# Split rows of both norms in two buffers each, queries' split moved to step 3, shared expert's down product in plain fp32

## The chip, the cores and the metric

The kernel runs on one core of a Trainium2 chip, written instruction by instruction with explicit semaphores. The metric is device time in microseconds, less is better.

## The reference

A layer without learned weights in its first norm feeds two branches, whose results are added to the input x (8 batches of 256 tokens of 128 values, fp32):

```python
xn = layernorm(x)
x + attention(xn) + ffn(xn)
# attention: a second layernorm with norm_g, norm_b; q from it, k and v from xn;
#   16 heads of 64, q and k scaled to unit length, 2 null keys and values a head,
#   a distance bias by head, causal mask, softmax, product with v, output projection Wout
# ffn: shared = (silu(xt @ sg_w.T) * (xt @ su_w.T)) @ sd_w.T       (128 -> 256 -> 128)
#   routed: sigmoid router, the 2 best of 8 experts, each 128 -> 256 -> 128
```

## The kernel before, in words

A preparation makes the norms, the router and the sorting of tokens by expert (32 scatters by GpSimd), and turns all weights. `xn1T` holds the first norm's result and `xn2T` the second's, both turned so that tokens lie along the free axis, complete before the main loop. Then 39 tiles of 128 routed tokens go through the experts. Then comes the attention loop, one entry per batch: `first` (batch 0), six times `mid`, `last`, and a short `drain`. The loops are unrolled; every engine runs its own copy of `entry(part, b, steps)` in a fixed order with 16 steps, one per head: in step s the scores of head s, the row maxima (DVE L900), the exponentials (ACT L676), the division (DVE L915), the transposes of the probabilities (PE L1111) and so on for heads some steps back.

Between them stand the side jobs, listed by hand in `JOBS` as (step, whose, kind, c, w, t) for two side banks. `kq` makes a half of the queries (w = 1, from `xs2`) or keys (w = 0, from `xs1`) of the next batch, `v` the values, `tr` transposes scaled queries and keys (PE L1066), `sh` is the shared expert's gate and up product, `yt` and `pn` close the batch before. The queries' first product (`kq`, w = 1) stands in step 1, the keys' and values' of the next batch in steps 5, 6, 12 to 15, the values' second half and `sh` of the own batch in steps 4, 5 and 8.

Many products use reduced-precision fp32 (`F32R`) in three matmuls: each operand is split into a rounded upper part and the remainder, and `three` (L969 to L973) adds hi x hi, lo x hi and hi x lo. The split of a batch's rows is two GpSimd instructions of 128x256, a cast and a subtraction (L457 and L460). Before, each of `xs1` and `xs2` has one buffer, so GpSimd makes both in steps 0 (xn2T, the queries) and 1 (xn1T) of the entry before, after the last product that reads the old content. As the own batch still needs xn1T in steps 4 to 8, step 2 splits it once more into `xs_late` (L477, L480). The shared expert's hidden rows `hs` are split in steps 7 and 10 (L468, L470) into `hss`, and the down product of step 13 (PE, after the output projection L1134) accumulates six matmuls into bank 6.

GpSimd also takes the inverse norms of queries and keys (a power of 128x8, L426 or L429), scales the rows by them (L442), copies the null probabilities (L495) and, in step 10, issues four gathers of expert outputs (L506). DVE adds these in the `yt` job (L870, L877). Semaphores count: `xhi` and `xlo` the parts of a split, `filled` and `left` the use of the side banks, `sh_h` the halves of `hs`.

Of the kernel before, what the change touches and what calls it, by code (L numbers as in the profile page):

```python
# [40 lines left out]
def build(nc, a, out):  # L41


    with ExitStack() as ctx:
        def sb(name, shape, dt=F32):
            return ctx.enter_context(nc.sbuf_tensor(name, shape, dt))
# [17 lines left out]
        sd = [sb("sd_hi", [P, 2, DIM], F32R), sb("sd_lo", [P, 2, DIM], F32R)]  # L64
# [57 lines left out]
        arena_r = sb("arena_r", [P, 3072], F32R)  # L122
# [6 lines left out]
        xs1, xs2 = ([carve_r(SEQ), carve_r(SEQ)] for _ in range(2))  # L129
        mxT = [[carve_r(P), carve_r(P)] for _ in range(RH)]  # L130
        mhT = [sb(f"mhT{i}", [P, I]) for i in range(2)]
        rt[0] = 4 * SEQ
        oT = [sb(f"oT{i}", [P, SEQ]) for i in range(2)]
        hss = [carve_r(2 * I), carve_r(2 * I)]
# [8 lines left out]
        xs_late = [sb(f"xs_late{i}", [P, SEQ], F32R) for i in range(2)]  # L143
# [9 lines left out]
        def three_d(n, m):  # L153
# [47 lines left out]
            "xhi", "xlo", "late_hi", "late_lo", "ksq", "red", "ssm_ready", "pw", "r_ready", "kqn",  # L201
            "sh_th", "sh_a", "sh_h", "sh_hi", "sh_lo", "shd",
# [87 lines left out]
        def head_at(part, s, lag):  # L290
# [12 lines left out]
                    [t[:].rearrange("p c d -> p (c d)") for t in sd], "d")]  # L303
# [6 lines left out]
        def settled(eng):  # L310


            eng.sem_inc(g.passed, 1)
# [48 lines left out]
        def _(pool):  # L362
# [80 lines left out]

            def entry(part, b, steps=range(HEADS)):
                whose = PARTS[part]
                nb = b + 1
                for s in steps:
                    if s < 2 and "next" in whose and part != "ready":
                        xT, xs = ((xn2T, xs2), (xn1T, xs1))[s]
                        for _, _, (kind, c, w, t, i, n) in (x for lag in range(1, HEADS) for x in behind(part, b, s, lag)):  # L450
                            if (kind, c, w, t) == (("kq", 1, 1, 1), ("v", 0, 0, 1))[s]:
                                pool.wait_ge(filled[i], n + 1)
                        if part == "first":
                            for i in range(2):
                                pool.wait_ge(filled[i], count("ahead", i) + count("ready", i))
                        settled(pool)
                        gp.tensor_copy(xs[0], xT[:, bass.ds(nb * SEQ, SEQ)]).then_inc(g.xhi, 1)  # L457
                        pool.wait_ge(g.xhi, 2 * nb + s + 1)
                        settled(pool)
                        gp.tensor_tensor(xs[1], xT[:, bass.ds(nb * SEQ, SEQ)], xs[0].bitcast(F32),  # L460
                                         ALU.subtract).then_inc(g.xlo, 1)
                    if s in (7, 10) and "own" in whose:
                        c = (7, 10).index(s)
                        pool.wait_ge(g.sh_h, 2 * b + c + 1)
                        if part != "first":
                            pool.wait_ge(g.shd, b)
                        settled(pool)
                        gp.tensor_copy(hss[0][:, c * SEQ:(c + 1) * SEQ], hs[:, c, :]).then_inc(g.sh_hi, 1)  # L468
                        pool.wait_ge(g.sh_hi, 2 * b + c + 1)
                        gp.tensor_tensor(hss[1][:, c * SEQ:(c + 1) * SEQ], hs[:, c, :],  # L470
                                         hss[0][:, c * SEQ:(c + 1) * SEQ].bitcast(F32), ALU.subtract).then_inc(g.sh_lo, 1)
                    if s == 2 and "own" in whose:
                        for _, _, (kind, c, _, t, i, n) in (x for lag in range(1, HEADS) for x in behind(part, b, s, lag)):
                            if (kind, c) == ("sh", 1):
                                pool.wait_ge(filled[i], n + 1)
                        settled(pool)
                        gp.tensor_copy(xs_late[0][:], xn1T[:, bass.ds(b * SEQ, SEQ)]).then_inc(g.late_hi, 1)  # L477
                        pool.wait_ge(g.late_hi, b + 1)
                        settled(pool)
                        gp.tensor_tensor(xs_late[1][:], xn1T[:, bass.ds(b * SEQ, SEQ)], xs_late[0][:].bitcast(F32),  # L480
                                         ALU.subtract).then_inc(g.late_lo, 1)
                    h = head_at(part, s, 2)
                    for _, job_b, job in (behind(part, b, s, 1) if part != "ahead" else []):
                        norms(job_b, job)
                        scale_by_norm(job_b, job)
                    if h is not None and h % 2:
                        p = h // 2
                        pool.wait_ge(g.pn, TB * (HEADS * b + h + 1))
                        if p == 0 and part != "first":
                            pool.wait_ge(g.pn_hi, 2 * b)  # L490
                        settled(pool)
                        q = p % PAIRS
                        two = prob[:, (HEADS * b + h) % RP - 1:(HEADS * b + h) % RP + 1, :]
# [35 lines left out]
        def _(act):  # L529
# [42 lines left out]
            sc.activation(xs1[0], xn1T[:, 0:SEQ], ACT.Copy).then_inc(g.xhi, 1)  # L572
# [6 lines left out]
            for i in range(8, 12):  # L579
                turned_out(i)  # L580
                if i == 8:
                    act.wait_ge(g.t_ev, 9)
                    sc.activation(xs2[0], xn2T[:, 0:SEQ], ACT.Copy).then_inc(g.xhi, 1)
# [140 lines left out]
        def _(dve):  # L724
# [86 lines left out]
            ve.tensor_tensor(xs1[1], xn1T[:, 0:SEQ], xs1[0].bitcast(F32), ALU.subtract).then_inc(g.xlo, 1)  # L811
# [16 lines left out]
            ve.tensor_tensor(xs2[1], xn2T[:, 0:SEQ], xs2[0].bitcast(F32), ALU.subtract).then_inc(g.xlo, 1)  # L828
# [137 lines left out]
        def _(pe):  # L966
# [82 lines left out]
            def side_job(job, b):  # L1049
# [7 lines left out]
                if kind == "kq":  # L1057
                    pe.wait_ge(g.xlo, 2 if isinstance(b, int) and b < 0 else 2 * nb + 2 - w)
                    ins = three(side[i][:], [x[:, tt] for x in (xs2 if w else xs1)],
                                [x[:, c * 512:(c + 1) * 512] for x in (wq if w else wkv)], True, True)  # L1060
# [6 lines left out]
                if kind == "v":  # L1067
                    if c:
                        pe.wait_ge(g.late_lo, b + 1)
                    else:  # L1070
                        pe.wait_ge(g.xlo, 2 * nb + 2)
                    ins = three(side[i][:], [x[:, tt] for x in (xs_late if c else xs1)],
                                [x[:, INNER + c * 512:INNER + (c + 1) * 512] for x in wkv], True, True)
                if kind == "sh":
                    pe.wait_ge(g.late_lo, b + 1)
                    for gu in range(2):
                        ins = three(side[i][:, gu * SEQ:(gu + 1) * SEQ],
                                    [x[:, (2 * gu + c) * P:(2 * gu + c + 1) * P] for x in sgu], [x[:] for x in xs_late], True, True)
# [10 lines left out]
            def entry(part, b, steps=range(HEADS)):  # L1089
                whose = PARTS[part]  # L1090
                for s in steps:
# [135 lines left out]
```

## Time and profile before

| | |
|---|---|
| median of 3 runs | 491.92 us (491.72 to 493.71) |
| profiled execution | 492.31 us, its span 490.6 us |
| PE / PEld | 86% / 62% of the span |
| DVE / ACT / POOL | 74% / 73% / 65% |
| share of the chain that ended last | PE 35%, POOL 24%, DVE 19%, issue 11%, ACT 7%, DMA 2% |

The profile records one execution. PE is TensorE's matmul, PEld its weight load, DVE VectorE, ACT ScalarE, POOL GpSimd. "x" is the number of instructions; of a plain fp32 matmul two records are shown. The ends of matmuls are modelled, so they can overlap by some tenths of a microsecond. A row of the timeline gives start and length in us, engine, line, operation, the tile written and those read; in brackets the idle time before it and what ended it. arena_b, arena_r and bank are names of storage that several tiles share.

### The profile page before, as it was taken

How to read it: one execution, taken by the hardware profiler on the slowest of the kernel's cores; microseconds unless marked ns; L12 is line 12 of the kernel's file. 1: busy time of each engine (PE TensorE's matmuls, PEld its weight loads, DVE VectorE, ACT ScalarE, POOL GpSimd, SP SyncE). 2: the span in 40 equal slices, each digit the busy share in tenths (PEclk: the TensorE clock that was granted, in tenths of full speed). 3: DMA queues.
4: the chain of work that ended last, by engine and by line, in shares of the span. 5: the costliest groups of instructions: out<-in, count | busy, mean ns of one | idle time of the engine just before them, and what ended most of it. 6: DMA issues, size and time to landing. Idle time of an engine off the chain costs nothing.

```text
span 490.6 us, 10747 instructions
## 1 busy us (share of the span) xinstructions
PE 423.7 (86%) x2809; PEld 306.4 (62%) x2809; DVE 363.6 (74%) x1419; ACT 358.9 (73%) x1098; POOL 319.9 (65%) x492
## 2 busy tenths in 40 slices
PE   4746807999997997999899899989999998999995
PEld 3734405777775775767666676766667676767663
DVE  5699604666644996798789779878978986997894
ACT  3354703666667986889897798989779798979874
POOL 3748779800005789498867959886795988778150
PEclk9969856999999999899999999999999999999999
DMA  8961111222220000000001000000100000010010
GB/s 236 321 227 33 54 53 49 76 82 81 79 62 16 1 18 6 3 23 21 3 1 35 11 1 24 21 3 2 37 8 2 22 23 3 1 38 7 2 43 13
DMA packets 29739, 21.37 MB, mean 44 GB/s; under 512 B 3528, under 2 KB 27376, under 8 KB 29552
## 3 DMA queue, kind: packets, MB, share of 16 engines
q1 hardware_dynamic: 26816, 16.46, 11.4%
q0 software_dynamic: 2048, 4.20, 2.9%
q8 instruction: 25, 0.41, 0.3%
q14 instruction: 34, 0.28, 0.2%
q10 hardware_dynamic: 816, 0.03, 0.1%
HBM read 12.41 MB, written 8.26 MB: 42 GB/s over the span
## 4 chain that ended last, share of the span: by engine, by line
PE 35%; POOL 24%; DVE 19%; issue 11%; ACT 7%; DMA 2%; ACTq 1%; DVEq 0%; POOLq 0%; SPq 0%
POOL slot_x L416 7%; PE bank L971 5%; DVE arena_b L900 5%; POOL rnorm L426 5%; PE bank L1190 4%; PE bank L1120 4%; PE bank L972 4%; PE bank L973 4%; POOL arena_b L506 4%; DVE arena_b L915 3%; PE bank L1111 3%; DVE arena_b L877 3%; POOL rpow L429 2%; POOL arena_b L442 2%; PE bank L1134 2%
## 5 line engine op out<-in xcount | busy, mean ns | idle before, releaser
L676 ACT ACTIVATE arena_b<-arena_b,nmx 128x130 f32<-128x130 f32 (+1 forms) x256 | 114.7, 456 | 17.4 <-DVE nmx L900 14.8
L900 DVE CUSTOM_DVE_ANT_0 arena_b<-bank,bias 128x130 f32<-128x130 f32 (+1 forms) x256 | 81.1, 354 | 37.5 <-ACT arena_b L676 20.9
L915 DVE TENSOR_SCALAR arena_b<-arena_b,rden 128x130 f32<-128x130 f32 (+1 forms) x256 | 78.5, 354 | 4.5
L429 POOL TENSOR_TENSOR rpow<-ssm,mhalf 128x8 f32<-128x8 f32 x32 | 52.9, 1653 | 36.2 <-DVE ssm L888 35.5
L1111 PE MATMUL bank<-ident,arena_b 128*128 128x128 f32 x384 | 67.4, 285 | 5.6 <-DVE arena_b L915 5.6
L442 POOL TENSOR_TENSOR arena_b<-arena_b,rnorm 128x512 f32<-128x512 f32 x64 | 66.9, 1045 | 5.0
L1120 PE MATMUL bank<-arena_a 64*128 64x130 f32 (+1 forms) x512 | 60.2, 354 | 0.8 <-ACT arena_a L637 0.8
L1111 PEld LDWEIGHTS bank<-ident,arena_b 128*128 128x128 f32 x384 | 44.1, 142 | 24.9 <-DVE arena_b L915 14.4
L884 DVE TENSOR_REDUCE ssq<-arena_b 128x8 f32<-128x512 f32 x64 | 43.7, 683 | 13.2 <-ACT arena_b L614 12.4
L426 POOL TENSOR_TENSOR rnorm<-ssm,mhalf 128x8 f32<-128x8 f32 x32 | 52.5, 1641 | 0.0
L676 ACT ACTIVATION_READ_ACCUMULATOR arena_b<-arena_b,nmx 128x1 f32 x256 | 50.8, 199 | 0.0
L614 ACT ACTIVATE arena_b<-bank 128x512 f32<-128x512 f32 x64 | 38.3, 598 | 16.5 <-PE bank L973 15.1
L416 POOL DMA_INDIRECT slot_x<-arena_a,slot x32 | 34.3, 1071 | 15.5 <-issue 9.3
L1101 PE MATMUL bank<-probT,arena_a 128*64 128x256 f32 x256 | 42.2, 404 | 2.1 <-DVE probT L925 1.3
L1066 PE MATMUL bank<-ident,arena_b 128*128 128x128 f32 x256 | 39.8, 279 | 2.8 <-ACT arena_a L627 1.1
L1120 PEld LDWEIGHTS bank<-arena_a 64*128 64x128 f32 x512 | 34.0, 188 | 12.5 <-issue 9.0
L506 POOL DMA_INDIRECT arena_b<-slot_y,slot_now x32 | 31.3, 977 | 13.8 <-POOL w_now L501 6.4
L925 DVE COPY probT<-bank 128x384 f32<-128x384 f32 x64 | 35.3, 552 | 4.9 <-DVE arena_b L854 2.1
L1134 PE MATMUL bank<-oT,wo 128*128 128x256 f32 x128 | 38.7, 384 | 0.0
L1066 PEld LDWEIGHTS bank<-ident,arena_b 128*128 128x128 f32 x256 | 29.4, 140 | 14.4 <-issue 3.3
L457 POOL CAST arena_r<-xn2T 128x256 fp32r<-128x256 f32 x7 | 2.9, 412 | 54.2 <-PE bank L973 54.2
L615 ACT ACTIVATE arena_b<-bank 128x512 f32<-128x512 f32 x64 | 38.2, 597 | 0.0
(209 smaller groups left out, 1030.3 us busy)
## 6 DMA issues: line engine op xcount, KB each, us to landing
slot_x<-probT SPq DMA_DIRECT2D x3, 832.0 KB, 8.6
arena_b<-slot_x SPq DMA_DIRECT2D x39, 64.0 KB, 1.9
slot_y<-arena_b SPq DMA_DIRECT2D x39, 64.0 KB, 1.5
arena_a<-in_L_attn_x_dram SPq DMA_DIRECT2D x2, 512.0 KB, 5.2
arena_b<-in_L_ffn_wd_dram SPq DMA_DIRECT2D x1, 1024.0 KB, 9.8
arena_b<-in_L_attn_Wkv_dram SPq DMA_DIRECT2D x1, 1024.0 KB, 8.5
arena_b<-in_L_attn_x_dram SPq DMA_DIRECT2D x8, 128.0 KB, 2.3
out_dram<-arena_b SPq DMA_DIRECT2D x8, 128.0 KB, 1.9
```

Source lines behind the costliest of these rows:

```text
L416: pool.indirect_dma_start(xg_dram, bass.IndirectOffsetOnAxis(ap=slot[:, n // TOPK, n % TOPK:n % TOPK + 1], axis=0), xn1[:, n // TOPK, :], ...
L426: gp.tensor_tensor(rnorm[:, j, :], ssm[:, j, :], mhalf[:, 0:HEADS // 2], ALU.pow).then_inc(g.r_ready, 1)
L429: gp.tensor_tensor(rpow[:, j, :], ssm[:, j, :], mhalf[:, 0:HEADS // 2], ALU.pow).then_inc(g.pw, 1)
L442: gp.tensor_tensor(rows, rows, bc(rnorm[:, j, :], DH), ALU.mult).then_inc(g.kqn, 1)
L506: pool.indirect_dma_start(yg[:, t, c, :], None, yg_dram, bass.IndirectOffsetOnAxis(ap=slot_now[:, t, c:c + 1], axis=0)).then_inc(g.gath, 16)
L676: sc.activation(prob[:, (HEADS * b + h) % RP, c], sim[h % 2][:, c], ACT.Exp, scale=-1.0, bias=nmx[:, h % HEADS, t:t + 1], accum_out=den[:, ...
L900: ve.tensor_tensor_reduce(out=sim[h % 2][:, c], in0=bank[h % 2][:, c], in1=bias[:, c], scale=-SLOPES[h], scalar=3e38, op0=ALU.add, op1=ALU ...
L915: ve.tensor_scalar(pr, pr, rden[:, h % HEADS, t:t + 1], None, ALU.mult).then_inc(g.pn, 1)
L1066: ins = te.transpose(side[i][:, q * P:(q + 1) * P], src[:, p * P:(p + 1) * P], ident[:])
L1111: ins = te.transpose(bank[2 + h % 2][:, k * P:(k + 1) * P], prob[:, (HEADS * b + h) % RP, c:c + P], ident[:])
L1120: ins = te.matmul(bank[half][:, c0:c1], qT[r, h // 2, q0:q0 + P], kT[r, h // 2, 0:c1 - c0], start=True, stop=True)
L1134: te.matmul(bank[6][:, 0:SEQ], wo[:, p % PAIRS, :], oT[p % 2][:], start=p == 0, stop=p == -1).then_inc(g.oread, 1)
```

## The change

The rows of both norms get a second buffer each, by parity of the batch. The queries' split for batch b+2 is made in step 3 of entry b (for batch 1 in step 0 of the first entry); that of the keys and values stays in step 1 for the next batch, and loses its wait for the values' product. `xs_late` and its split go; the values' second half and `sh` read `xs1[b % 2]`. `sd` is kept whole in fp32, `hs` is no longer split, and the down product is two plain fp32 matmuls instead of six. The new buffers lie where the experts' turned inputs `mxT` were.

```diff
-        sd = [sb("sd_hi", [P, 2, DIM], F32R), sb("sd_lo", [P, 2, DIM], F32R)]
+        sd = sb("sd", [P, 2, DIM])
...
-        xs1, xs2 = ([carve_r(SEQ), carve_r(SEQ)] for _ in range(2))
+        xs1, xs2 = ([[carve_r(SEQ), carve_r(SEQ)]] for _ in range(2))
...
         rt[0] = 4 * SEQ
+        for ring in (xs1, xs2):
+            ring.append([carve_r(SEQ), carve_r(SEQ)])
-        hss = [carve_r(2 * I), carve_r(2 * I)]
-        xs_late = [sb(f"xs_late{i}", [P, SEQ], F32R) for i in range(2)]
...
+            def split_for_queries(n):
+                xs, cols = xs2[n % 2], bass.ds(n * SEQ, SEQ)
+                gp.tensor_copy(xs[0], xn2T[:, cols]).then_inc(g.xhi, 1)
+                pool.wait_ge(g.xhi, 2 * n + 1)
+                gp.tensor_tensor(xs[1], xn2T[:, cols], xs[0].bitcast(F32), ALU.subtract).then_inc(g.xlo, 1)
...
+                    if s == 0 and part == "first":
+                        split_for_queries(1)
+                    if s == 1 and "next" in whose and part != "ready":
                         for _, _, (kind, c, w, t, i, n) in (x for lag in range(1, HEADS) for x in behind(part, b, s, lag)):
                             if (kind, c) == ("sh", 1):
                                 pool.wait_ge(filled[i], n + 1)
+                        xs, cols = xs1[nb % 2], bass.ds(nb * SEQ, SEQ)
+                        gp.tensor_copy(xs[0], xn1T[:, cols]).then_inc(g.xhi, 1)
+                        pool.wait_ge(g.xhi, 2 * nb + 2)
+                        gp.tensor_tensor(xs[1], xn1T[:, cols], xs[0].bitcast(F32), ALU.subtract).then_inc(g.xlo, 1)
...
+                    if s == 3 and "next" in whose and nb + 1 < BATCH:
+                        for _, _, (kind, c, w, t, i, n) in (x for lag in range(1, HEADS) for x in behind(part, b, s, lag)):
+                            if (kind, c, w, t) == ("kq", 1, 1, 1) and part != "first":
+                                pool.wait_ge(filled[i], n + 1)
+                        split_for_queries(nb + 1)
...
                     if s == 13 and "own" in whose:
-                        pe.wait_ge(g.sh_lo, 2 * b + 2)
+                        pe.wait_ge(g.sh_h, 2 * b + 2)
                         for c in range(2):
-                            ins = three(bank[6][:, 0:SEQ], [x[:, c, :] for x in sd], [x[:, c * SEQ:(c + 1) * SEQ] for x in hss],
-                                        False, False)
-                        ins.then_inc(g.shd, 1)
+                            te.matmul(bank[6][:, 0:SEQ], sd[:, c, :], hs[:, c, :], start=False, stop=False)
```

## Rows read from the trace of the kernel before

**Rows 1.** The page: busy time of each engine, share of the span, instructions.

```profile
PE 423.7 (86%) x2809; PEld 306.4 (62%) x2809; DVE 363.6 (74%) x1419; ACT 358.9 (73%) x1098; POOL 319.9 (65%) x492
```

**Rows 2.** Busy time in stretches of one batch each; columns in first line.

```profile
core 0: us, PE busy (x) PEld busy (x) DVE busy (x) ACT busy (x) POOL busy (x), PEclk, DMA share, GB/s
...
280.50:323.20 42.70, 40.17 (x283) 28.59 (x283) 35.51 (x147) 36.24 (x114) 34.12 (x52) 1.00 0.05 14
```

**Rows 3.** Waits of the whole execution: total us, times, longest us.

```profile
PE bank L971 <- POOL arena_r L460: 9.0, 6, 2.7
...
PE bank L1111 <- DVE arena_b L915: 5.6, 7, 0.9
```

**Rows 4.** TensorE in order of time around step 1, two batches (start, length).

```profile
279.47 0.55 PE L1111 MATMUL bank<-ident,arena_b 128*128 128x128 f32 x3
281.47 0.47 PE L971 MATMUL bank<-wq_hi,arena_r 128*128 128x512 f32 x1 [1.46 <-POOL arena_r L460]
...
194.51 0.47 PE L971 MATMUL bank<-wq_hi,arena_r 128*128 128x512 f32 x1 [2.65 <-POOL arena_r L460]
```

**Rows 5.** TensorE in order of time, step 1 of the last three entries.

```profile
367.64 0.60 PE L1066 MATMUL bank<-ident,arena_b 128*128 128x128 f32 x4
...
409.57 0.47 PE L971 MATMUL bank<-wq_hi,arena_r 128*128 128x512 f32 x1 [1.24 <-POOL arena_r L460]
...
410.35 0.60 PE L1066 MATMUL bank<-ident,arena_b 128*128 128x128 f32 x4
...
450.48 0.55 PE L1111 MATMUL bank<-ident,arena_b 128*128 128x128 f32 x3
450.87 0.60 PE L1066 MATMUL bank<-ident,arena_b 128*128 128x128 f32 x4
```

**Rows 6.** GpSimd in order of time, steps 15 to 0.

```profile
278.65 1.04 POOL L442 TENSOR_TENSOR arena_b<-arena_b,rnorm 128x512 f32<-128x512 f32 x1
...
280.03 0.39 POOL L457 CAST arena_r<-xn2T 128x256 fp32r<-128x256 f32 x1
280.60 0.72 POOL L460 TENSOR_TENSOR arena_r<-xn2T,arena_r 128x256 fp32r<-128x256 f32 x1 [0.18 <-POOL arena_r L457]
```

**Rows 7.** GpSimd's longest pause in a batch.

```profile
291.92 1.64 POOL L429 TENSOR_TENSOR rpow<-ssm,mhalf 128x8 f32<-128x8 f32 x1 [4.40 <-DVE ssm L888]
```

**Rows 8.** ScalarE and VectorE in order of time, the same stall.

```profile
282.45 0.60 ACT L614 ACTIVATE arena_b<-bank 128x512 f32<-128x512 f32 x1 [1.94 <-PE bank L973]
...
283.08 0.69 DVE L884 TENSOR_REDUCE ssq<-arena_b 128x8 f32<-128x512 f32 x1 [1.21 <-ACT arena_b L614]
...
284.69 0.29 DVE L900 CUSTOM_DVE_ANT_0 arena_b<-bank,bias 128x130 f32<-128x130 f32 x1 [0.55 <-PE bank L1120]
```

**Rows 9.** TensorE in order of time at step 13, the down product.

```profile
228.43 0.60 PE L1134 MATMUL bank<-oT,wo 128*128 128x256 f32 x2
...
229.58 0.49 PE L1111 MATMUL bank<-ident,arena_b 128*128 128x128 f32 x3
...
255.08 0.59 PE L1134 MATMUL bank<-oT,wo 128*128 128x256 f32 x2
255.51 0.49 PE L1111 MATMUL bank<-ident,arena_b 128*128 128x128 f32 x3
```

**Rows 10.** VectorE in order of time, steps 7 to 9 of one batch.

```profile
298.53 0.91 DVE L915 TENSOR_SCALAR arena_b<-arena_b,rden 128x130 f32<-128x130 f32 x2
...
299.92 2.05 DVE L877 SCALAR_TENSOR_TENSOR arena_b<-arena_b,w_now 128x128 f32<-128x128 f32 x4 [0.16 <-DVE arena_b L870]
...
303.55 0.55 DVE L915 TENSOR_SCALAR arena_b<-arena_b,rden 128x130 f32<-128x130 f32 x2
```

**Rows 11.** GpSimd in order of time, steps 7 and 8 of the same batch.

```profile
298.36 0.73 POOL L470 TENSOR_TENSOR arena_r<-arena_b,arena_r 128x256 fp32r<-128x256 f32 x1
...
300.76 1.06 POOL L442 TENSOR_TENSOR arena_b<-arena_b,rnorm 128x512 f32<-128x512 f32 x1
```

**Rows 12.** Busy time and granted clock right after the longest stall.

```profile
193.30:210.00 16.70, 15.49 (x97) 11.11 (x97) 10.30 (x42) 12.88 (x39) 10.02 (x19) 0.90 0.01 2
```

More of the change, by code:

```diff
@@ L119, in build @@
         probT = [sb(f"probT{i}", [P, 3 * P]) for i in range(2)]
-        arena_r = sb("arena_r", [P, 3072], F32R)
+        arena_r = sb("arena_r", [P, 2048], F32R)
         rt = [0]
@@ L199, in build @@
             "m_xps", "m_xhi", "m_xlo", "m_gups", "m_th", "m_ga", "m_h", "m_hps", "m_hT", "m_yps", "m_yev",
-            "xhi", "xlo", "late_hi", "late_lo", "ksq", "red", "ssm_ready", "pw", "r_ready", "kqn",
-            "sh_th", "sh_a", "sh_h", "sh_hi", "sh_lo", "shd",
+            "xhi", "xlo", "ksq", "red", "ssm_ready", "pw", "r_ready", "kqn",
+            "sh_th", "sh_a", "sh_h",
             "sps", "ttr", "exp", "rd", "pn", "ptps", "ptev_a", "ptev_d", "pvd", "oev", "oread",
@@ L302, in build @@
                    ([raw_sd[:, c * P:(c + 1) * P] for c in range(2)],
-                    [t[:].rearrange("p c d -> p (c d)") for t in sd], "d")]
+                    [sd[:].rearrange("p c d -> p (c d)")], "d")]
         EARLY = 4
@@ L447, in entry @@
                 for s in steps:
-                    if s < 2 and "next" in whose and part != "ready":
-                        xT, xs = ((xn2T, xs2), (xn1T, xs1))[s]
+                    if s == 0 and part == "first":
+                        split_for_queries(1)
+                    if s == 1 and "next" in whose and part != "ready":
                         for _, _, (kind, c, w, t, i, n) in (x for lag in range(1, HEADS) for x in behind(part, b, s, lag)):
[L451 to L471, printed above, removed]
@@ L472, in entry @@
-                    if s == 2 and "own" in whose:
-                        for _, _, (kind, c, _, t, i, n) in (x for lag in range(1, HEADS) for x in behind(part, b, s, lag)):
                             if (kind, c) == ("sh", 1):
                                 pool.wait_ge(filled[i], n + 1)
[L476 to L481, printed above, removed]
+                        xs, cols = xs1[nb % 2], bass.ds(nb * SEQ, SEQ)
@@ L571, in _ @@
                 turned_out(i)
-            sc.activation(xs1[0], xn1T[:, 0:SEQ], ACT.Copy).then_inc(g.xhi, 1)
+            sc.activation(xs1[0][0], xn1T[:, 0:SEQ], ACT.Copy).then_inc(g.xhi, 1)
             for n in range(EARLY):
@@ L582, in _ @@
                     act.wait_ge(g.t_ev, 9)
-                    sc.activation(xs2[0], xn2T[:, 0:SEQ], ACT.Copy).then_inc(g.xhi, 1)
+                    sc.activation(xs2[0][0], xn2T[:, 0:SEQ], ACT.Copy).then_inc(g.xhi, 1)
             for n in range(EARLY, len(groups)):
@@ L810, in _ @@
             dve.wait_ge(g.xhi, 1)
-            ve.tensor_tensor(xs1[1], xn1T[:, 0:SEQ], xs1[0].bitcast(F32), ALU.subtract).then_inc(g.xlo, 1)
+            ve.tensor_tensor(xs1[0][1], xn1T[:, 0:SEQ], xs1[0][0].bitcast(F32), ALU.subtract).then_inc(g.xlo, 1)
             for n in range(EARLY):
@@ L827, in _ @@
             dve.wait_ge(g.xhi, 2)
-            ve.tensor_tensor(xs2[1], xn2T[:, 0:SEQ], xs2[0].bitcast(F32), ALU.subtract).then_inc(g.xlo, 1)
+            ve.tensor_tensor(xs2[0][1], xn2T[:, 0:SEQ], xs2[0][0].bitcast(F32), ALU.subtract).then_inc(g.xlo, 1)
             dve.wait_ge(g.wraw_hi, 2)
@@ L1058, in side_job @@
                     pe.wait_ge(g.xlo, 2 if isinstance(b, int) and b < 0 else 2 * nb + 2 - w)
-                    ins = three(side[i][:], [x[:, tt] for x in (xs2 if w else xs1)],
+                    ins = three(side[i][:], [x[:, tt] for x in (xs2 if w else xs1)[nb % 2]],
                                 [x[:, c * 512:(c + 1) * 512] for x in (wq if w else wkv)], True, True)
@@ L1067, in side_job @@
                 if kind == "v":
[L1068 to L1072, printed above, removed]
+                    pe.wait_ge(g.xlo, 2 * (b if c else nb) + 2)
+                    ins = three(side[i][:], [x[:, tt] for x in xs1[(b if c else nb) % 2]],
                                 [x[:, INNER + c * 512:INNER + (c + 1) * 512] for x in wkv], True, True)
                 if kind == "sh":
-                    pe.wait_ge(g.late_lo, b + 1)
+                    pe.wait_ge(g.xlo, 2 * b + 2)
                     for gu in range(2):
                         ins = three(side[i][:, gu * SEQ:(gu + 1) * SEQ],
-                                    [x[:, (2 * gu + c) * P:(2 * gu + c + 1) * P] for x in sgu], [x[:] for x in xs_late], True, True)
+                                    [x[:, (2 * gu + c) * P:(2 * gu + c + 1) * P] for x in sgu], xs1[b % 2], True, True)
                 if kind == "pn":
```

## The prediction

> **What bounds the kernel now.** I began with the page. TensorE (PE) is the busiest engine with 86% of the span, VectorE (DVE) and ScalarE (ACT) follow at about 74%, GpSimd (POOL) has 65% [rows 1]. These are averages over a preparation, an expert stage and the attention loop, and the change touches only the loop. So I took busy times of one batch: of 42.7 us TensorE is busy 40.2, ScalarE 36.2, VectorE 35.5 and GpSimd 34.1, at the full 2.4 GHz clock [rows 2]. TensorE is the resource nearest to its limit, and what stops it is what counts. The view of waits names two repeated stops of TensorE in the loop: six times it waits, 9.0 us in all, at L971 for the subtraction at L460, and seven times 0.8 us on average, 5.6 in all, at L1111 for L915 [rows 3]. The first is the queries' product of step 1 waiting for the lower half of the split of xn2T, which GpSimd makes in step 0. There are seven entries with a next batch and six such waits: the first entry has none.
>
> Why is GpSimd late? From step 10 on it works through the gathers, three norm chains and two splits with hardly a pause: it ends its last scaling at 279.69 and only then starts the cast at 280.03 and the subtraction at 280.60, which TensorE awaits from 280.0 on, when its transposes are through (279.47 + 0.55) [rows 4, 6]. It is late by its place in the order, not by lack of time: in step 4 of the same batch it idles 4.40 us [rows 7].
>
> **What a stall costs.** The row shows 1.46 us of idle time, 2.65 in the second batch [rows 4], but the modelled ends of matmuls hide a bit. The last entry is a natural trial: it has neither this split nor this product. From the L1066 of step 1 to the same instruction a batch later 42.71 us pass (367.64 to 410.35) with the stall, and 40.52 (410.35 to 450.87) without [rows 5]. The product itself takes 0.78 us of that (409.57 to 410.35). So the stall costs 42.71 - 40.52 - 0.78 = 1.41 us where the row says 1.24: 0.17 is hidden. Six stalls: 9.0 + 6 x 0.17 = 10.0 us.
>
> Does the time come back at the next wait? ScalarE idles 1.94 us in this stall, and VectorE 1.21 and then 0.55 for the next scores [rows 8]. Both have at least the 1.41 us to give before they hold TensorE, VectorE with 1.76 - 1.41 = 0.35 to spare. In the last entry the L1066 follows the transposes before it at the pace of work, 0.39 us after their start, so nothing else stands right behind the stall [rows 5]. I count all 10.0.
>
> **Part 1, two buffers and the split a batch ahead.** The queries' split of batch b+2 now runs in step 3 of entry b, before GpSimd's 4.40 us pause, and reads xn2T, which has been complete since the preparation. Cast and subtraction take 0.39 + 0.72 = 1.11 us [rows 6], so the pause covers them three times over. Behind them in GpSimd's order stand the norms of the product of step 4, for which it pauses anyway. Their own wait, for the product of step 11 of the entry before, was met long ago, since the split is three steps later than the old one. Without that cover, 1.11 us would be added to the chain to the norms of step 4. The keys' and values' split stays in step 1 and is used from step 5 on, four steps of 2.7 us (42.7 / 16) later. The new buffers lie over the experts' transposed inputs; GpSimd waits for the experts' outputs before the first entry anyway, and no DMA is issued, added or moved past another. Gain: 10.0 us.
>
> **Part 2, no late split.** One cast and subtraction, 1.11 us of GpSimd a batch by the same rows, go; the values' second half and the shared expert read the kept buffer. TensorE's matmuls are the same. It is worth nothing on TensorE's path: that split was done before step 3 and used in step 4 or later.
>
> **Part 3, down product in plain fp32.** GpSimd loses two more splits of the same size (0.73 us for a subtraction, 0.39 for a cast, 2.2 us a batch) [rows 6, 11], and the product waits for hs itself, which is earlier. On TensorE six reduced-precision matmuls give way to two plain ones. The two output projection matmuls at L1134 and the six of the down product take 1.15 us from start to start (228.43 to 229.58); the same L1134 alone takes 0.43 (255.08 to 255.51), and its two records are the two halves of one plain fp32 matmul of 256 columns [rows 9]. So six take 0.72 us and two plain ones 2 x 0.43 = 0.86: TensorE gets 0.14 us **more** work a batch, 8 x 0.14 = 1.1 us. Bounds: 0, should the switch between kinds of matmul cost the 0.14, and 1.1.
> The Trainium skill speaks against this part too: its page "FP8 and Floating Point Precision", section TensorE Precision Notes, gives true fp32 four passes, so eight passes would replace six. By that the product would go from 0.72 to 0.96 us, an estimate, and cost 1.9 us in all; no row shows the two side by side in one place, and the row of L1134 makes it less.
> In the preparation the two groups sd_hi and sd_lo become one copy; no step on its path hangs on that, and I count 0.
>
> **Part 4, GpSimd out of VectorE's way.** In steps 7 and 8 VectorE is behind and TensorE waits for it, 0.8 us a batch [rows 3]. There L915's pair takes 0.91 us at 298.53, while the subtraction L470 runs from 298.36 to 299.09, and 0.55 at 303.55 with no such neighbour [rows 10, 11]. L470 goes, and 0.36 us a batch could return. The four L877 take 2.05 us, with L442 beside them from 300.76 [rows 10, 11]. L442 now comes about 1 us sooner and still meets them or the end of L870, so I don't count on that. Bounds: 0 if another GpSimd instruction takes L470's place, and all 5.6 us if the whole wait at L1111 goes. I take half of 0.36, seven times: 1.3 us, near the lower bound, since L442 is the longer neighbour and stays.
> The Trainium skill, page "SBUF — State Buffer", section Who interferes with whom, has GpSimd and VectorE share a port pair that one of them holds for a whole instruction. By that rule the L877 (two SBUF inputs) stay blocked wherever L442 catches them, or are free if it doesn't. The first gives my sum, the second the rival below.
>
> **The sum.** 10.0 - 1.1 + 1.3 = 10.2 us. The profiled execution took 492.31 us (span 490.6); 492.31 - 10.2 = 482.1, and the median of the runs is 0.39 lower: **481.7 us**.
>
> **The rivals.**
> - *The stall goes whole* (my forecast): 481.7 us, its own range 479.5 to 484. Chance 0.62.
> - *VectorE takes over as the bound.* It has only 0.35 us to spare behind the old stall. If the moved split's 0.72 us subtraction now blocks a VectorE instruction on that stretch, 1.76 - 0.72 = 1.04 us a batch is left to gain: five times that plus 2.1 for the long stall, less 1.1, is 6.2 us (the 2.1 is 2.65 + 0.17 - 0.72): 485.7. For it: the stretched L915 [rows 10]. Against: the split sits in a part where VectorE waits for others. Chance 0.17.
> - *VectorE is freed as well*, L442 slips past the L877, and the wait of 0.8 us a batch goes: 491.92 - 10.0 + 1.1 - 5.6 = 477.4. A smaller form: in the stretch right after the 2.65 us stall the granted clock was 0.90 on average over 16.7 us, so a fifth of it, 3.3 us, ran at 1.2 GHz, which costs up to 1.7 us; a later batch shows 1.00 [rows 2, 12]. Without the stall these 1.7 us may go too: 480.0. Chance of something of this kind beyond my own range 0.13.
> - *The wait only moves*: GpSimd is as late at another point, the scaled queries and keys that steps 0 to 3 transpose. The last of them was scaled at 279.69 and TensorE needs it in step 3, two steps of 2.7 us after the product at 281.47 [rows 4, 6], so the slack is over 5 us and the 1.41 doesn't use it up. If it were so, 492. Chance 0.04.
> - *Slower*: the two splits that remain, 1.11 us each, now block VectorE where it has no slack, twice a batch: 7 x 2.2 = 15.5 us against 8.9 gained gives 498.5. It turns the sign from 1.27 us a batch. Against it: such splits run today as well and the longest stretch seen in these rows is 0.36 us for one. Chance 0.04.
>
> The range takes the forecast, the second rival and most of the third: 477.6 to 486.3. A measurement of this kernel tells about 0.5% (2.5 us) from nothing. Faster by more than that: 0.91; within: 0.05; slower: 0.04.
>
> **What would show it.** In the profile after, no row of L971 waiting for GpSimd; TensorE's batch from step 1 to step 1 of 41.3 us or less instead of 42.7; GpSimd's busy time a batch down from 34.1 to about 30.8; two plain matmuls 0.86 us long at step 13; the wait at L1111 for L915 still there at 0.5 to 0.9. A batch of 42 us or more with VectorE named in longer waits at L1111 would show the second rival, and would make the prediction wrong.

## The result and the profile after

The kernel after takes 479.31 us (median of 6 runs, 479.1 to 480.74), the kernel before 492.62 us beside it (6 runs, 491.04 to 493.87): ratio 0.9735, 95% interval 0.9711 to 0.9759, or 13.3 us less. The forecast was 481.7 with a range of 477.6 to 486.3.

The lines of the kernel after have new numbers: `three` is L958 to L960 (was L971 to L973), the transposes of the probabilities L1095 (L1111), the division L902 (L915), the additions of the experts' rows L864 (L877), the queries' split L446 and L448, the scaling still L442. Busy times of the page after, to be read against [rows 1]:

```profile
PE 422.1 (88%) x2793; PEld 305.4 (64%) x2793; DVE 365.5 (76%) x1419; ACT 359.1 (75%) x1097; POOL 295.6 (62%) x444
```

GpSimd has 48 instructions and 24.3 us less, TensorE 16 matmul records less (six reduced matmuls a batch give way to two plain ones of two records each). The view of waits of the kernel after, TensorE's own rows (us in all, times, longest), against [rows 3]:

```profile
PE bank L1146 <- DMA arena_b<-slot_x: 18.5, 4, 17.4
...
PE bank L1095 <- DVE arena_b L902: 4.4, 7, 0.7
...
PE bank L1053 <- ACT arena_a L614: 1.1, 2, 0.8
```

The 9.0 us in which TensorE waited for GpSimd in the loop are gone; no such row is left (the view's one row with GpSimd, 4.8 us, belongs to the preparation). The largest row belongs to the experts' stage ahead of the loop. The wait for the division stays, smaller: 4.4 us for 5.6. Busy times by batch of the kernel after (first batch, the next two, and the one that stands for all later ones, against [rows 2]):

```profile
154.71:193.02 38.31, 36.84 (x263) 26.25 (x261) 33.50 (x144) 35.20 (x111) 30.06 (x44) 1.00 0.03 8
193.02:234.04 41.02, 40.03 (x284) 28.55 (x283) 35.84 (x147) 36.48 (x114) 31.80 (x47) 1.00 0.06 15
234.04:275.09 41.05, 40.06 (x285) 28.56 (x283) 36.23 (x147) 36.51 (x114) 31.34 (x47) 1.00 0.05 14
275.09:316.11 41.02, 40.03 (x284) 28.56 (x283) 36.22 (x147) 36.47 (x114) 31.31 (x47) 1.00 0.05 15
```

and the same four of the kernel before:

```profile
152.80:194.51 41.71, 37.20 (x264) 26.21 (x263) 36.31 (x151) 35.92 (x113) 34.24 (x50) 1.00 0.03 8
194.51:238.54 44.03, 41.65 (x283) 29.59 (x284) 35.01 (x146) 36.69 (x113) 34.13 (x53) 0.96 0.05 14
238.54:281.47 42.93, 40.21 (x283) 28.59 (x284) 35.60 (x147) 36.46 (x113) 34.36 (x53) 1.00 0.05 14
281.47:324.17 42.70, 40.17 (x283) 28.59 (x284) 35.51 (x147) 36.45 (x113) 34.13 (x53) 1.00 0.05 14
```

The columns are the length of the stretch, the busy time of PE, PEld, DVE, ACT and POOL with the number of instructions, the granted clock, the DMA engines' busy share and GB/s. Each stretch runs from one queries' product of step 1 to the next, so a stall in front of the product counts to the stretch that it ends. A batch is 3.40, 3.01, 1.88 and then 1.68 us shorter (the two that follow, 42.70 to 41.02 and to 41.04, are like the fourth): 13.3 us over the six. In the second batch TensorE's busy time falls by 1.62 us, in the fourth by 0.14: the matmuls of [rows 12] that ran at the lower clock run at full speed now. The tail from the last queries' product to the end is 0.3 us shorter; the preparation and the experts' stage are 1.9 us longer in this execution, which was the longest of the six.

### The profile page after: what moved, and what is told of

Read it like the earlier page. It is cut to its first block, busy times and chain, and to the rows that moved or that the text cites. A ratio compares the mean times of both kernels' runs of the same rounds, so it can differ in the third digit from the quotient of the medians.

```text
span 478.9 us, 10606 instructions
## 1 busy us (share of the span) xinstructions
PE 422.1 (88%) x2793; PEld 305.4 (64%) x2793; DVE 365.5 (76%) x1419; ACT 359.1 (75%) x1097; POOL 295.6 (62%) x444
## 4 chain that ended last, share of the span: by engine, by line
PE 58%; DVE 17%; POOL 7%; issue 7%; ACT 6%; DMA 4%; DVEq 0%; SPq 0%; ACTq 0%
PE bank L1104 8%; PE bank L1095 7%; POOL slot_x L416 7%; PE bank L958 7%; PE bank L959 5%; PE bank L960 5%; PE bank L1085 5%; PE bank L1053 4%; PE bank L1118 4%; DVE arena_b L887 4%; PE bank L1172 4%; DMA arena_b<-slot_x 3%; DVE arena_b L864 3%; DVE arena_b L902 2%; PE bank L1086 2%
## 5 line engine op out<-in xcount | busy, mean ns | idle before, releaser
L902 DVE TENSOR_SCALAR arena_b<-arena_b,rden 128x130 f32<-128x130 f32 (+1 forms) x256 | 81.5, 364 | 4.5
L442 POOL TENSOR_TENSOR arena_b<-arena_b,rnorm 128x512 f32<-128x512 f32 x64 | 68.0, 1062 | 5.0
L1095 PE MATMUL bank<-ident,arena_b 128*128 128x128 f32 x384 | 67.0, 283 | 4.4 <-DVE arena_b L902 4.4
L1104 PE MATMUL bank<-arena_a 64*128 64x130 f32 (+1 forms) x512 | 59.5, 351 | 0.8 <-ACT arena_a L624 0.8
L1095 PEld LDWEIGHTS bank<-ident,arena_b 128*128 128x128 f32 x384 | 44.2, 141 | 24.0 <-DVE arena_b L902 12.8
L1104 PEld LDWEIGHTS bank<-arena_a 64*128 64x128 f32 x512 | 33.6, 186 | 12.2 <-issue 9.0
L1118 PE MATMUL bank<-oT,wo 128*128 128x256 f32 x128 | 38.2, 381 | 0.0
L477 POOL COPY pnull<-arena_b 128x4 f32<-128x4 f32 x128 | 22.0, 201 | 25.7 <-DVE arena_b L902 25.6
```

The lines of the kernel that those rows point to most:

```text
L442: gp.tensor_tensor(rows, rows, bc(rnorm[:, j, :], DH), ALU.mult).then_inc(g.kqn, 1)
L902: ve.tensor_scalar(pr, pr, rden[:, h % HEADS, t:t + 1], None, ALU.mult).then_inc(g.pn, 1)
L1095: ins = te.transpose(bank[2 + h % 2][:, k * P:(k + 1) * P], prob[:, (HEADS * b + h) % RP, c:c + P], ident[:])
L1104: ins = te.matmul(bank[half][:, c0:c1], qT[r, h // 2, q0:q0 + P], kT[r, h // 2, 0:c1 - c0], start=True, stop=True)
L1118: te.matmul(bank[6][:, 0:SEQ], wo[:, p % PAIRS, :], oT[p % 2][:], start=p == 0, stop=p == -1).then_inc(g.oread, 1)
```

## The experiments

Twelve runs in three sets; the kernels of a set ran together beside runs of before of their own, whose medians were 498.09, 499.44 and 493.01 us. Ratios compare within a set. In the first two sets the kernel before and every version of the kernel after are slower than in the traces above; what is different there is told below, and it hid most of what the first set was to show. The third set gives the first result again.

### One part at a time (first set)

```diff
 # q_split_only: the kernel before, and of the change only this
+xs2.append([carve_r(SEQ), carve_r(SEQ)])
+                    if s == 3 and "next" in whose and nb + 1 < BATCH:
...
+                        split_for_queries(nb + 1)
```


> The kernel before with the queries' split alone changed: two buffers for the rows of xn2T, split in step 3 a batch ahead. The late split, the split of hs and the six matmuls of the down product stay. If the stall came from the split's place in GpSimd's order, it goes whole: about 1.5 us a batch in six batches, and the 1.2 GHz stretch behind the longest stall: 480 to 483 us. The rival, that GpSimd's load made the stall and only less work for it helps, gives 488 us or more.


```diff
 # down_fp32_only: the kernel before, and of the change only this
-                    if s in (7, 10) and "own" in whose:
...
-                        gp.tensor_copy(hss[0][:, c * SEQ:(c + 1) * SEQ], hs[:, c, :]).then_inc(g.sh_hi, 1)
...
+                            te.matmul(bank[6][:, 0:SEQ], sd[:, c, :], hs[:, c, :], start=False, stop=False)
```


> The kernel before with the down product alone in plain fp32 and no split of hs. GpSimd's unbroken run from step 8 to step 0 is one split (1.1 us) shorter, so the stall of 1.4 us at L971 should shrink to about 0.3 us, while TensorE gets 0.14 us a batch more: 485 to 488 us. If the stall depended on the place alone and not on the load, no gain: 492 to 494 us.


```diff
 # after_hs_split_kept: the kernel after, with the split of hs and the six matmuls of before
+                    if s in (7, 10) and "own" in whose:
...
+                            ins = three(bank[6][:, 0:SEQ], [x[:, c, :] for x in sd], [x[:, c * SEQ:(c + 1) * SEQ] for x in hss],
+                                        False, False)
```


> The changed kernel with the split of hs and the six reduced-precision matmuls back. TensorE has 0.14 us a batch less work (1.1 us in all), VectorE meets one more GpSimd subtraction in step 7 (0.2 us a batch at the wait at L1095): 479 us, between 477.5 and 480.5. If the plain product is cheaper than I priced it, or the relief of GpSimd was worth more, it is slower than the changed kernel by 2 us or more.


```diff
 # after_q_split_step0: the kernel after, with the queries' split for the next batch back in step 0
+                    if s == 0 and "next" in whose and part != "ready":
...
+                        split_for_queries(nb)
-                        split_for_queries(nb + 1)
```


> The changed kernel with two buffers kept, but the queries' split back in step 0 for the next batch. GpSimd has one split less before it (that of hs in step 10), so it ends its last scaling about 1.1 us sooner, and the stall comes back at some 0.2 to 0.5 us a batch: 480.5 to 482.5 us. If the load alone had made the stall, no loss: 479.3.

Measured, against 498.09 us:

| kernel | us | ratio (95%) | a later batch, us |
|---|---|---|---|
| q_split_only | 494.04 | 0.991 (0.9876 to 0.9945) | 42.03 to 42.76 |
| down_fp32_only | 493.17 | 0.9899 (0.9839 to 0.996) | 42.39 to 42.44 |
| after_hs_split_kept | 493.54 | 0.9893 (0.9865 to 0.9922) | 41.55 to 42.68 |
| after_q_split_step0 | 492.24 | 0.987 (0.9812 to 0.9928) | 42.38 to 42.46 |

All four are about 1% faster than before and none can be told from another: their intervals overlap. The forecasts of times (479 to 488 us) failed: in the traces VectorE or ScalarE takes a result of TensorE late once in nearly every batch, as told in the second set, and the kernel before was itself 5.5 us slower here than in the first result. The traces still answer one question. None of the four has a row in which TensorE waits for GpSimd in the loop, not even the two in which the queries' split is still made in step 0. GpSimd (first fence) and TensorE (second) in order of time, after_q_split_step0:

```profile
319.80 0.45 POOL L480 COPY pnull<-arena_b 128x4 f32<-128x4 f32 x2
320.19 0.39 POOL L446 CAST arena_r<-xn2T 128x256 fp32r<-128x256 f32 x1
320.67 0.72 POOL L448 TENSOR_TENSOR arena_r<-xn2T,arena_r 128x256 fp32r<-128x256 f32 x1
```
```profile
322.10 0.55 PE L1093 MATMUL bank<-ident,arena_b 128*128 128x128 f32 x3
322.40 0.48 PE L956 MATMUL bank<-wq_hi,arena_r 128*128 128x512 f32 x1
```

The subtraction is through at 321.39 and TensorE comes for it at 322.40: a microsecond early, where TensorE had waited 1.2 to 1.5 us for it in [rows 4, 5]. Two things do that. GpSimd works almost without a pause from the gathers to this subtraction, and one split of hs less stands in front of them: counted from the queries' product a batch before, the subtraction ends at 41.39 us here, with 0.49 us of waiting for VectorE in it, and at 42.55 in the batch of the kernel before that ends at 324.17. And TensorE itself comes only at 42.40 instead of 41.0, by the lateness told below. Without it the wait would be between none and 0.4 us, an estimate from these numbers: the lighter GpSimd takes away most of the stall, whether all of it was not tried.

### The kernel after and before again, and the price of the down product (second set)

> The changed kernel once more, unchanged, as the control for the other kernels of this call, since the kernel before took 498 us in the last call and 492 before. If the smaller gains of the four kernels of that call were their own, this one again takes 0.973 of the kernel before. If they were the chip's, this one too gains less, and its profile shows the same waits without a releaser on ScalarE and VectorE.

> The kernel before once more, for its profile beside the others of this call: its batch takes 42.7 us if the chip is as in the first profile, more if the chip adds waits of its own.

Measured, against 499.44 us: after_again 494.02, ratio 0.9882 (0.9832 to 0.9932), batches of 42.45 us; before_again 498.33, ratio 0.9981 (0.9949 to 1.0013), batches of 42.79 to 42.90. The change is worth 5.4 us here and not 13.3. The kernel before loses 0.1 to 0.2 us a batch against [rows 2], the kernel after 1.42. TensorE, VectorE and ScalarE in order of time, after_again, steps 10 to 12:

```profile
309.62 0.93 PE L1104 MATMUL bank<-arena_a 64*128 64x130 f32 x8
310.48 0.51 PE L958 MATMUL bank<-wkv_hi,arena_r 128*128 128x512 f32 x1
...
314.32 0.50 PE L958 MATMUL bank<-wkv_hi,arena_r 128*128 128x512 f32 x1 [1.15 <-ACT arena_b L602]
```
```profile
310.74 0.18 DVE L875 TENSOR_SCALAR ssm<-ssq 128x8 f32<-128x8 f32 x1
313.31 0.29 DVE L887 CUSTOM_DVE_ANT_0 arena_b<-bank,bias 128x130 f32<-128x130 f32 x1 [2.39 <-remote]
```
```profile
313.18 0.60 ACT L601 ACTIVATE arena_b<-bank 128x512 f32<-128x512 f32 x1 [0.94 <-remote]
313.68 0.59 ACT L602 ACTIVATE arena_b<-bank 128x512 f32<-128x512 f32 x1
```

The scores (L1104) end at 310.55, and VectorE, which needs nothing else, takes them at 313.31 only; the values' product ends about 311.4, and ScalarE takes it at 313.18. Both start within 0.13 us of each other, which reads as if TensorE's completions had reached them late, together; the trace names no instruction for it. TensorE then waits 1.15 us for ScalarE at the next product. In the trace of the first result the same pair of the kernel after stands without a gap:

```profile
303.92 0.18 DVE L875 TENSOR_SCALAR ssm<-ssq 128x8 f32<-128x8 f32 x1
304.12 0.29 DVE L887 CUSTOM_DVE_ANT_0 arena_b<-bank,bias 128x130 f32<-128x130 f32 x1
```

In the kernel before, TensorE is 0.80 us later at step 13 in this set (L1134 stands 33.41 us behind the product of step 1 for 32.61), and the stall at the end of the same batch is 0.67 us shorter (0.57 for 1.24; in all 3.8 us in four waits for 9.0 in six): most of the lateness falls into time that it lost anyway.

```diff
 # after_six_matmuls: six reduced-precision matmuls on rows that are split already, in place of the two plain ones
...
-                            te.matmul(bank[6][:, 0:SEQ], sd[:, c, :], hs[:, c, :], start=False, stop=False)
+                            three(bank[6][:, 0:SEQ], [x[:, c, :] for x in sd], xs1[b % 2], False, False)
```


> The changed kernel with six reduced-precision matmuls in place of the two plain ones, taken over the split rows of xn1T in place of hs, so that no split of hs is needed (another product than the reference's). GpSimd and VectorE work as in the changed kernel. TensorE has 0.14 us a batch less: 1.1 us faster than the changed kernel. By four passes for a plain matmul against one it would be 1.9 us; if the change between kinds of matmul costs as much as the passes, the same time.

Measured: 492.69 us, ratio 0.9856 (0.9806 to 0.9907), 1.33 us less than after_again, and 42.28 us a batch for 42.45: 0.17 where 0.14 had been worked out. The intervals of the two ratios overlap; the four times of each (492.19 to 492.95, 493.78 to 494.22) don't, and the batches, which repeat within a trace to 0.06 us, carry the verdict. Two plain matmuls cost more TensorE time than six reduced ones.

```diff
 # after_second_add_later: the kernel after, the second expert's addition at the end of step 9
...
+                    if s == SECOND and "prev" in whose and part != "drain":
+                        second_expert(b)
```


> The changed kernel with the second expert's addition of the batch before (two of the four L864) at the end of step 9 on VectorE instead of in step 8. If TensorE's wait of 0.7 us at L1095 is VectorE's backlog from these additions, it shrinks by up to 0.7 us a batch, 3 to 5 us in all; if VectorE is late all the way, the wait moves to step 10 and the time stays within 1 us.

Measured: 488.95 us, ratio 0.978 (0.973 to 0.9829), 5.1 us less than after_again, with batches of 41.7 us (one of 42.02). That is more than the 3.8 us by which the wait it was to remove fell (5.1 to 1.3), and VectorE has no late row between 200 and 430 us here, where after_again has five of 2.4 us. So part of it comes from the lateness, and the run was made again.

### Without the lateness (third set)

> The kernel after once more, unchanged, beside the three runs that follow. If this chip is like the first, its loop has batches of 41.0 us and the ratio is 0.973; if it is like the second and third, batches of 42.4 us, with VectorE and ScalarE each waiting some 2.4 and 0.9 us once a batch for a TensorE instruction that was long done, and the ratio is 0.988.

> The kernel before with the queries' buffers and their split in step 3 alone, this time beside the kernel after on one chip. If each part hides the same 1.4 us stall, it lies within 1.5 us of the kernel after, above or below; if the parts add up, it is 3 us or more slower than the kernel after.

> The kernel after with the second expert's addition moved on VectorE from step 7 to the end of step 9, beside the unchanged one on the same chip. If VectorE's lateness at the transposes of steps 7 to 9 holds TensorE, as the 0.7 us waits say, it is again 4 to 6 us faster than the unchanged kernel after, with a batch of 0.6 to 0.8 us less; if the gain of the first run came from the late completions of that chip alone, it is under 1.5 us on a chip that has none.


```diff
 # after_gathers_once: the gathers of the experts' rows for the first batch only
-                        for t in range(TB):
+                        for t in range(TB if b == 0 else 0):
...
-                    dve.wait_ge(g.gath, 16 * TB * TOPK * b)
+                    dve.wait_ge(g.gath, 16 * TB * TOPK)
```


> Leaves out the four gathers of the experts' rows in seven of the eight batches; the additions use the first batch's rows, so the output is another one. Theory A: TensorE's completions are told late, once a batch, because the gathers are being issued; then the late waits in steps 10 to 12 are gone and the batch is 41.0 us where the kernel after has 42.4 on this chip (on a chip without the late waits both have 41.0). Theory B: the lateness has nothing to do with the gathers; then a batch stays within 0.3 us of that of the unchanged kernel after, for GpSimd, which is all that gets less work, holds nothing up in it.

Measured, against 493.01 us:

| kernel | us | ratio (95%) | batches from the fourth on, us |
|---|---|---|---|
| after_third | 479.96 | 0.9728 (0.968 to 0.9776) | 41.05 |
| q_split_only_2 | 483.26 | 0.9796 (0.9758 to 0.9833) | 41.54 |
| after_second_add_later_2 | 477.55 | 0.967 (0.963 to 0.971) | 40.67 |
| after_gathers_once | 479.38 | 0.9712 (0.9672 to 0.9751) | 41.03 |

The queries' buffers and split alone bring 9.75 us, and the rest of the change 3.3 us on top, so it does more than take away the same stall. What the rest brings alone was not run in this set, so the two shares hold in this order only. TensorE's rows with idle time before them in a later batch of q_split_only_2, of after and of after_second_add_later_2 (there L1104 are the transposes; in q_split_only_2 it is L1124, and the division L928):

```profile
280.23 0.66 PE L1079 MATMUL bank<-ident,arena_b 128*128 128x128 f32 x4 [0.15 <-ACT arena_a L636]
297.74 0.55 PE L1124 MATMUL bank<-ident,arena_b 128*128 128x128 f32 x3 [0.90 <-DVE arena_b L928]
301.07 0.55 PE L1124 MATMUL bank<-ident,arena_b 128*128 128x128 f32 x3 [0.25 <-DVE arena_b L928]
```
```profile
297.43 0.55 PE L1095 MATMUL bank<-ident,arena_b 128*128 128x128 f32 x3 [0.69 <-DVE arena_b L902]
```
```profile
279.12 0.66 PE L1062 MATMUL bank<-ident,arena_b 128*128 128x128 f32 x4 [0.15 <-ACT arena_a L611]
298.95 0.55 PE L1104 MATMUL bank<-ident,arena_b 128*128 128x128 f32 x3 [0.22 <-DVE arena_b L909]
```

The 0.15 us for ScalarE is in every kernel: these transposes start 5.19 or 5.20 us behind the product of step 1 in the traces of before, q_split_only_2 and after alike, and the view shows the wait only where it reaches 0.15. The wait of 0.25 us stands in all six batches of q_split_only_2 and in none of before, beside the 0.90 that was there already [rows 3]. Without the splits of hs and the late one it is gone, and the 0.90 is 0.69. Its cause shows on VectorE (first fence) and GpSimd (second), q_split_only_2:

```profile
292.10 0.91 DVE L928 TENSOR_SCALAR arena_b<-arena_b,rden 128x130 f32<-128x130 f32 x2
...
299.91 1.11 DVE L928 TENSOR_SCALAR arena_b<-arena_b,rden 128x130 f32<-128x130 f32 x2
```
```profile
291.93 0.73 POOL L478 TENSOR_TENSOR arena_r<-arena_b,arena_r 128x256 fp32r<-128x256 f32 x1
...
300.14 0.72 POOL L478 TENSOR_TENSOR arena_r<-arena_b,arena_r 128x256 fp32r<-128x256 f32 x1
```

Both subtractions of hs lie on a division that the next transposes wait for, and its pair takes 0.91 and 1.11 us instead of 0.55. In the kernel before they lay on both as well, but at the second it was GpSimd that gave way. VectorE (first fence) and GpSimd (second), kernel before:

```profile
306.33 0.55 DVE L915 TENSOR_SCALAR arena_b<-arena_b,rden 128x130 f32<-128x130 f32 x2
```
```profile
306.57 0.90 POOL L470 TENSOR_TENSOR arena_r<-arena_b,arena_r 128x256 fp32r<-128x256 f32 x1
```

The subtraction starts 0.24 us after the pair here and 0.23 in q_split_only_2, so the moved split did not shift the two against each other. In six of six batches of before the pair keeps its 0.55 us and the subtraction takes 0.90; in six of six of q_split_only_2 it is 1.11 and 0.73; in q_split_only, the same program in the first set, the pair keeps its 0.55 in all six; in after_hs_split_kept four pairs of six take 1.11. Which of the two gives way can thus turn with the start times equal to 0.02 us; what tips it stays open.

after_second_add_later_2 is 2.4 us faster than after_third in the medians and 1.9 between the first and the last of the seven products: the wait before the transposes falls from 0.70 to 0.22 and a batch from 41.05 to 40.67. The forecast of 4 to 6 us was wrong, and more than half of the second set's 5.1 us is not this wait. The intervals of the two ratios overlap, but its four times (476.19 to 477.9) lie below all four of after_third (478.31 to 481.72): it is the fastest version here.

after_gathers_once left the batch at 41.03. In this set after_third has no late completions with all its gathers either, so the run doesn't tell whether they cause them. It does show that 4.5 us less of GpSimd a batch (26.96 for 31.51) brings TensorE nothing more.

## Why the prediction was right

**What bounds the loop, and why GpSimd was late.** Right. TensorE's idle time in a later batch was 42.70 - 40.17 = 2.53 us and is 0.99 now; the row at the queries' product is gone, and the view shows no other wait of TensorE for GpSimd in the loop.

**Part 1, forecast 10.0 us.** Right in size, 9.75 in the medians and 9.8 over the loop, but as a sum of two errors. In the batches from the fourth on the queries' split alone brings 42.70 - 41.54 = 1.16 us and not 1.41. The stall itself was worth a little more than priced: counted from the product of step 1, TensorE runs within 0.02 us alike in before and q_split_only_2 as far as the transposes that wait 0.90 us, and those behind the second pair start at 25.71 us in before (307.18) and at 26.04 in q_split_only_2 (301.07). So 1.16 + 0.33 = 1.49 us of stall went, and 0.33 came back at one new wait for VectorE, of which the row shows 0.25. That is the second rival's kind of loss, near the 0.72 - 0.35 = 0.37 us it was priced at, but through a split of hs that gave way before, and not through the moved one. In q_split_only this pair was not stretched, so the loss does not belong to the move as such. In the total it was made up by the second batch, where the clock that [rows 12] show at 0.90 is now 1.00:

```profile
192.00:208.00 16.00, 15.86 (x116) 11.30 (x116) 14.07 (x59) 15.05 (x47) 10.60 (x20) 1.00 0.01 3
```

TensorE had stood idle 2.65 us just before that stretch [rows 4] and doesn't now. The second batch's busy time of 41.65 against 40.17 us later puts the price at 1.5 us, its length of 44.03 against 42.70, both with a stall of 1.2 us at their end, at 1.3; the prediction gave up to 1.7 and left it out of the sum, as a smaller form of the third rival.

**The moved split hides in GpSimd's pause.** Right. It runs at 281.31 to 282.52 and a pause of 3.02 us follows. It does stretch a division beside it, as the second rival feared, but there TensorE doesn't wait. VectorE (first fence) and GpSimd (second), kernel after:

```profile
281.56 1.11 DVE L902 TENSOR_SCALAR arena_b<-arena_b,rden 128x130 f32<-128x130 f32 x2
```
```profile
281.79 0.73 POOL L448 TENSOR_TENSOR arena_r<-xn2T,arena_r 128x256 fp32r<-128x256 f32 x1
285.54 1.64 POOL L429 TENSOR_TENSOR rpow<-ssm,mhalf 128x8 f32<-128x8 f32 x1 [3.02 <-DVE ssm L875]
```

**Part 3, forecast 1.1 us more.** Right. The plain product takes 308.64 - 307.78 = 0.86 us to the next transposes, TensorE in order of time:

```profile
307.34 0.60 PE L1118 MATMUL bank<-oT,wo 128*128 128x256 f32 x2
307.78 1.03 PE L1123 MATMUL bank<-arena_b,sd 128*128 128x256 f32 x4
308.64 0.49 PE L1095 MATMUL bank<-ident,arena_b 128*128 128x128 f32 x3
```

From L1118 that is 1.30 us where [rows 9] have 1.15, so 0.15 a batch, and after_six_matmuls gave 0.17 back (1.3 us in all). The Trainium skill, page "FP8 and Floating Point Precision", section TensorE Precision Notes, has plain fp32 at four passes, so eight in place of six. These rows don't show that ratio: the product grew by a fifth, from 0.72 to 0.86 us, not by a third. By [rows 9] a plain matmul of 256 columns takes 0.43 us from start to start and a reduced one 0.12 (0.72 for six), so 3.6 times as much.

**Part 4, forecast 1.3 us: the step that failed in size.** The term took half of 0.36 us a batch, "near the lower bound, since L442 is the longer neighbour and stays". The rest of the change is worth 3.3 us in the medians on top of part 1; with the 1.3 us of the down product added back, a lighter GpSimd is worth 4.6 us, or 0.66 a batch over seven. In a later batch the same comes out of the rows: 41.54 - 41.03 = 0.51 (0.49 against after_third), and 0.15 for the product, is 0.66. It stands at two places. Counted from the product of step 1, the transposes of the 0.90 us wait start at 22.71 us in q_split_only_2 and at 22.34 in after: 0.37, so the 0.36 us of the stretched division come back whole, not by half; that L442 stays took nothing from it. The other 0.3 is the 0.33 that had come back at the second pair in q_split_only_2, which the prediction didn't see. The division in front of the wait takes 0.55 us again, while the four additions are as slow as before, for L442 still lies on them, as expected. VectorE and GpSimd, kernel after:

```profile
292.15 0.55 DVE L902 TENSOR_SCALAR arena_b<-arena_b,rden 128x130 f32<-128x130 f32 x2
...
293.19 2.05 DVE L864 SCALAR_TENSOR_TENSOR arena_b<-arena_b,w_now 128x128 f32<-128x128 f32 x4 [0.16 <-DVE arena_b L857]
```
```profile
293.38 1.07 POOL L442 TENSOR_TENSOR arena_b<-arena_b,rnorm 128x512 f32<-128x512 f32 x1
```

In after_second_add_later_2 two of the additions stay beside L443 (its scaling) and two are made later without it; VectorE:

```profile
292.04 1.40 DVE L863 SCALAR_TENSOR_TENSOR arena_b<-arena_b,w_now 128x128 f32<-128x128 f32 x2 [0.16 <-DVE arena_b L858]
...
297.62 0.60 DVE L880 SCALAR_TENSOR_TENSOR arena_b<-arena_b,w_now 128x128 f32<-128x128 f32 x2
```

The pair costs 1.40 with the neighbour and 0.60 without. The Trainium skill, page "SBUF — State Buffer", section Who interferes with whom, has a VectorE instruction with two SBUF inputs, as these are, contend with a GpSimd instruction that reads SBUF, as L443 does; the runs agree with it.

**The total.** By the medians of the third set 9.75 for part 1, 4.6 for the lighter GpSimd, less 1.3 for the down product: 13.05, beside 13.3 in the first result. The rows make of part 1 about as much: 10.0 of stalls, 1.3 to 1.5 of clock, less 1.5 to 2.0 that came back at the second pair (six times 0.25 to 0.33). The sum of 10.2 us was thus 3 us short, and the forecast's own range ended at 479.5, 0.2 us above the result. The prediction had named both that carried it there, the clock and the relief of VectorE, but left the first out and halved the second.

**The rivals.** VectorE did not take over: the waits for it at the transposes are 4.4 us in all, less than before. Nor was it freed whole: 0.69 of 0.89 us a batch stay there, though the result lies beyond the forecast's own range on that rival's side. The wait did not move to another GpSimd product. No run was slower than before.

## What to carry over

Price a stall by a part of the same trace that lacks it, as the last entry did here: it gave 1.41 us, the runs show 1.49, and 1.16 came; then look for what a later wait takes back. Where two engines lie side by side and one has to give way, look at both, also where the critical one loses nothing now: here the same pair at the same distance cost GpSimd 0.2 us in one trace and VectorE 0.56 in another. And a share that a part of a change brings holds for the order in which the parts were taken.

## What the runs showed of the hardware

The same program took 479 us in the first result and the third set and 494 in the second, the kernel before 492 to 493 and 498 to 499. From the first to the last queries' product the kernel after takes 8.4 us more there, 1.42 in a later batch, and nearly all of that stands at one place: TensorE's results of steps 10 to 12 are taken by VectorE and ScalarE up to 2.8 us after they were through, both at nearly the same moment, while GpSimd issues the four gathers (307.26 to 312.17) and just after. The view of waits of after_again puts them down to a source it can't name:

```profile
ACT arena_b L601 <- remote: 19.1, 9, 3.9
...
DVE arena_b L887 <- remote: 16.4, 7, 2.5
```

Seven such waits of VectorE, and no row of either kind in the traces of the first result and of after_third. In before_again, where the first gather stands 27.05 us behind the product of step 1 and not 25.39 as in after_again, it is ScalarE alone that is late from the second batch on, by 0.4 to 1.1 us. Whether the gathers cause it stays open, since the run without them fell into a set that shows no lateness at all; so does what differed between the sets, the chip or its condition at the time (the first set ran on a chip numbered 7, the second and the third on one numbered 0, so the number doesn't part them). What it means for a measurement is plain: a gain of 13 us in one set was 5.4 us in another, with the same two programs.
